# The first four slots of an expert stage loaded ahead of its table, and table work placed between its first steps

## The reference, cut to what matters

```python
logits = xf @ router_w.T
probs = jax.nn.softmax(logits, axis=-1)
_, top_idx = jax.lax.top_k(probs, TOP_K)
...
g = jnp.einsum('td,efd->tef', xf, gate_w)
u = jnp.einsum('td,efd->tef', xf, up_w)
h = jax.nn.silu(g) * u
h = h * comb_w[:, :, None]
y = jnp.einsum('tef,edf->td', h, down_w)
return y.reshape(B, S, D) + residual
```

## Time and profile before

| | |
|---|---|
| median of 3 runs | 547.34 us (545.66 to 548.88) |
| the profiled execution | 546.67 us, its span 545.0 us |
| TensorE busy | 482.8 us, 89% of the span |
| VectorE busy | 375.4 us, 69% |
| ScalarE busy | 304.6 us, 56% |
| GpSimd busy | 194.4 us, 36% |
| mean granted clock | 0.969 of 2.4 GHz |

### The profile page before, as it was taken

The page is one execution under the profiler, slowest core; times in us unless marked ns, Lnnn a source line. Parts: engine busy times, 40 slices in busy tenths (PEclk is TensorE's granted clock), DMA queues, the critical chain, the costliest instruction groups (busy, mean ns, idle before and its releaser), DMA issues.

```text
span 545.0 us, 12569 instructions
## 1 busy us (share of the span) xinstructions
PE 482.8 (89%) x3157; PEld 459.7 (84%) x3158; DVE 375.4 (69%) x1293; ACT 304.6 (56%) x773; POOL 194.4 (36%) x280
## 2 busy tenths in 40 slices
PE   1999998999788987799999999999999999999900
PEld 1999997877576876789999999999999999999800
DVE  4969996359979988857665665665665655665597
ACT  5484967548588885435444444444444444444473
POOL 1000000005667777764333333333333333333330
PEclk9999999999899998899999999999999999999965
DMA  8988123811333342262222222222222222225897
GB/s 304 413 351 356 24 93 94 313 45 44 106 109 118 95 128 78 91 173 72 79 75 68 78 75 68 76 77 68 76 76 68 76 77 68 71 81 154 258 354 232
DMA packets 61695, 71.67 MB, mean 132 GB/s; under 512 B 19057, under 2 KB 55730, under 8 KB 60642
## 3 DMA queue, kind: packets, MB, share of 16 engines
q1 hardware_dynamic: 49920, 51.43, 30.5%
q0 software_dynamic: 8592, 17.75, 9.0%
q10 hardware_dynamic: 3154, 2.15, 1.2%
HBM read 49.43 MB, written 21.86 MB: 131 GB/s over the span
## 4 chain that ended last, share of the span: by engine, by line
PE 73%; DVE 14%; DMA 5%; ACT 4%; issue 2%; ACTq 1%; SPq 0%; DVEq 0%; POOL 0%; POOLq 0%
PE bank L839 8%; PE pair L839 6%; PE bank L1089 5%; PE bank L1085 5%; PE bank L1088 5%; PE bank L1087 5%; PE bank L1086 5%; PE bank L1096 5%; PE pair L1105 4%; PE bank L1105 4%; PE pair L984 4%; PE pair L1074 3%; PE pair L988 3%; ACT yall L743 2%; DMA ydram<-ysb,dnow 2%; PE bank L918 2%
## 5 line engine op out<-in xcount | busy, mean ns | idle before, releaser
L776 POOL DMA_INDIRECT disp<-xf,posu x82 | 83.6, 1019 | 151.9 <-ACT xf L654 124.9
L1576 DVE TENSOR_TENSOR hh<-sg,bank 128x384 f32<-128x384 f32 x89 | 49.3, 554 | 99.5 <-ACT sg L724 99.5
L813 POOL DMA_INDIRECT ydram<-ysb,dnow x89 | 88.2, 991 | 70.6 <-DMA ydram<-ysb,dnow 36.5
L724 ACT ACTIVATE sg<-bank 128x384 f32<-128x384 f32 x89 | 43.7, 491 | 116.9 <-PE bank L1089 116.9
L1085 PE MATMUL bank<-wa,xh 128*128 x178 | 67.5, 379 | 0.0
L1089 PE MATMUL bank<-wa,xl 128*128 x178 | 60.4, 340 | 0.0
L1088 PE MATMUL bank<-wa,xh 128*128 x178 | 59.9, 337 | 0.0
L1086 PE MATMUL bank<-wa,xh 128*128 x178 | 59.7, 336 | 0.0
L1087 PE MATMUL bank<-wa,xl 128*128 x178 | 59.7, 336 | 0.0
L810 POOL COPY dnow<-dest 128x1 uint32 (+1 forms) x89 | 16.4, 185 | 105.9 <-DVE ysb L1586 96.5
L839 PE MATMUL bank<-wcT,imgT 128*128 128x193 f32 x240 | 42.5, 340 | 11.1 <-DMA imgT<-in_pixels 11.1
(11 more groups left out here) (263 smaller groups left out, 1170.9 us busy)
## 6 DMA issues: line engine op xcount, KB each, us to landing
xs<-disp SPq DMA_DIRECT2D x89, 96.0 KB, 1.9
band<-in_bands SPq DMA_DIRECT2D x4, 1536.0 KB, 12.1
yall<-ydram SPq DMA_DIRECT2D x7, 768.0 KB, 7.1
imgT<-in_pixels SPq DMA_DIRECT2D x4, 768.0 KB, 12.8
imgT<-in_pixels SPq DMA_DIRECT2D x2, 1536.0 KB, 16.2
hres<-in_text SPq DMA_DIRECT2D x1, 3072.0 KB, 26.1
wa<-in_gate_up_w SPq DMA_DIRECT2D x8, 384.0 KB, 8.5
ring<-in_gate_up_w SPq DMA_DIRECT2D x32, 96.0 KB
```

The costliest lines, as they stand in the source:

```text
L776: pool.indirect_dma_start(disp, bass.IndirectOffsetOnAxis(ap=posu[c % XBUF][:, 2 * j + k:2 * j + k + 1], axis=0), xfd[c % XBUF][:, j, :], None
L813: pool.indirect_dma_start(ydram, bass.IndirectOffsetOnAxis(ap=dnow[b][:], axis=0), ysb[r][:], None).then_inc(s_ys[b], 16)
```

## The change

VectorE takes a decision in chunk 9: where expert 0 has 512 rows ahead of that chunk, its first four slots are full and their places known (rows 0, 128, 256 and 384). It writes three numbers into `first` and gives table signal 1. SyncE reads them, waits for the scatters of chunks 0 to 8 (or, where the rows are fewer, for all and for signal 2), reads four row numbers and a guard from `pre` with an offset that it has read, and loads slots 0 to 3. Later it waits for the rest, reads four row numbers and a guard, and loads slots 4 to 7; then it waits for signal 4, reads all eight numbers of `ready`, and goes into the loop.

TensorE does the transposes of slot 0 ahead of its throw-away products, which are 10 in place of 40, and ahead of the table, now signal 2. Its wait for the whole table, at step 5, is now for signal 4.

VectorE keeps only the first part of the table ahead of the steps. The softmax's first half goes into step -2, `MID` and `ready` (signal 3) into steps 0 to 2, `FAR` (signal 4) into steps 3 and 4, the softmax's second half into steps 5 to 8. ScalarE does the exponential and a table load between the first steps too.

```diff
-WARM = (10, 40)
+FIRST_ROWS = DEPTH * P
+FIRST_CHUNK = 9
+OTHER = 8
+WARM = (10, 10)
...
# SyncE
             sp.wait_ge(s_tab, 1)
-            begin = [sp.alloc_register(f"slot_row{s}") for s in range(GUARDED)]
-            sp.reg_load(begin, tab[0:1, 0, 0:GUARDED])
-            free = [sp.value_load(guard[0:1, g:g + 1], ...) for g in range(GUARDED // DEPTH)]
+            tables = sp.value_load(first[0:1, 0:1], min_val=1, max_val=2)
+            other = sp.value_load(first[0:1, 1:2], min_val=0, max_val=OTHER)
+            full = landed(FIRST_CHUNK, 0, 0)
+            lowers = sp.value_load(first[0:1, 2:3], min_val=full, max_val=full + 16)
             for p in range(XBUF):
                 for j in range(4):
...
+                        sp.wait_ge(s_scat[p][j], lowers)
+            sp.wait_ge(s_tab, tables)
+            begin = [sp.value_load(pre[0:1, bass.ds(other + s, 1)], ...) for s in range(DEPTH)]
+            free = sp.value_load(pre[0:1, bass.ds(other + DEPTH, 1)], ...)
+            sp.wait_ge(s_pool, free)
...
+            for s in range(DEPTH):
+                if s == 2:
+                    sp.wait_ge(s_rt, CHUNKS)
+                load_slot(s, s, begin[s])
...
             sp.wait_ge(s_pool, POOL_SETUP + 1)
-            sp.wait_ge(s_tab, 3)
+            sp.wait_ge(s_tab, 4)
+            done = [[sp.value_load(ready[0:1, f, b:b + 1], ...) for b in range(2)]
+                    for f in range(len(MARKS) + 2)]
             with sp.Fori(0, (SLOTS - GUARDED) // DEPTH) as i:
...
# ScalarE
-            act.wait_ge(s_w, 1)
-            nc.scalar.activation(top8[...], top8[...], ACT.Exp).then_inc(s_exp, 1)
-            nc.scalar.preload_act_table_set("silu_and_others")
...
+                if isinstance(k, int) and k == -2:
+                    nc.scalar.preload_act_table_set("exp_and_others")
+                if isinstance(k, int) and k == -1:
+                    act.wait_ge(s_w, 1)
+                    nc.scalar.activation(top8[...], top8[...], ACT.Exp).then_inc(s_exp, 1)
+                    nc.scalar.preload_act_table_set("silu_and_others")
...
# TensorE
-            keep_busy(bank[0], WARM[1])
-            pe.wait_ge(s_lo, UNITS)
-            pe.wait_ge(s_tab, 1)
...
-                if isinstance(k, int) and k in (1, 5):
-                    pe.wait_ge(s_tab, 2 if k == 1 else 3)
+                if isinstance(k, int) and k == 5:
+                    pe.wait_ge(s_tab, 4)
...
+                if isinstance(k, int) and k == -2:
+                    keep_busy(bank[0], WARM[1])
+                    pe.wait_ge(s_lo, UNITS)
+                    pe.wait_ge(s_tab, 2)
...
# VectorE, places(c)
+                if c == FIRST_CHUNK:
+                    before = bank[6][0:1, RK:RK + 1]
+                    st.mark(v.tensor_scalar(first[0:1, 0:1], before, float(FIRST_ROWS), 1.0, ALU.is_lt, ALU.add))
+                    st.link(v.tensor_scalar(first[0:1, 1:2], before, float(FIRST_ROWS), float(OTHER), ALU.is_lt, ALU.mult))
+                    v.tensor_scalar(first[0:1, 2:3], first[0:1, 1:2], 16.0 / OTHER, 96.0, ALU.mult, ALU.add).then_inc(s_tab, 1)
...
# VectorE, between(k)
-                if k == 0:
+                if k == 3:
                     experts(*FAR)
-                if k == 1:
+                if k == 4:
                     rows_of(*FAR).then_inc(s_tab, 1)
...
-            pipeline(v, step, "xght", (2, 1, 0, -1), peel=5)
+            pipeline(v, step, "xght", (2, 1, 0, -1), peel=7)
```

## The result

The change makes the kernel 1.1% slower: 553.35 us (median of 4 runs, 550.75 to 554.74) against 547.22 us for the kernel before in the same session. The ratio is 1.0106, with a 95% interval of [1.0056, 1.0156]. The profiled execution took 552.51 us with a span of 550.9 us, 5.9 us over the span of before; its mean granted clock is 0.953 for 0.969.

The account below looks back on a forecast made before the run. Bound: forty throw-away products between chunks and slots, then a full TensorE. Slot 8's transposes 6.9 us later plus 1.7 us of low clock make +8.6 us on the profiled 546.67: 555.3 us, range 550.8 to 559.0.

Parts of the forecast that it names:

- Part 1 and 2: Front: early loads of slots 0 to 3, ten throw-away products for forty; slot 1's transposes at 233.5, 1.7 us earlier.
- Part 3: VectorE's work moved between the first steps: +0.1 us in all, at most +0.8.
- Part 4: TensorE at step 5 waits for signal 4, which VectorE gives after step 4's far rows: it stands 2.85 us.
- Part 5: SyncE's eight reads between signal 4 and slot 8's load take 5.2 us; TensorE stands 5.65 us more.
- The rival by which reads are nearly free: SyncE's eight reads pass at the rate of its moves, slot 8 only 0.5 us late: 548.4 us, chance 0.07.
- The failed term: Steps behind slot 8's start run at 1.2 GHz for a while: +1.7 us, 0 if the clock holds.
- a slow step 5 costs nothing: Low clock behind TensorE's first gap, at step 5: no further cost, since that step ends ahead of slot 8.
- the prediction's own signs: Wrong if slots 7 to 8 take under 5 us, clock is 1.00 through the gap, or first loads issue after 227.
- The last rival: SyncE's reads at 0.28 us plus 0.15 per check, 3.5 us for eight, and no clock loss: 551.9 us, chance 0.06.

Follow-up runs that it names:

- e2: The kernel after, with SyncE and TensorE waiting for signal 3 instead of 4, the eight reads staying ahead of slot 8: 545.44 us, ratio 0.9952.
- e3: e2 with the eight reads of `ready` moved behind the slot loop: 546.63 us, ratio 0.9974.
- e6: e2 with slots 8 to 11 written out and one pair of reads of `ready` behind each: 545.38 us, ratio 0.9954.
- e7: e6 with four row numbers in one register load, for slots 0 to 3 and again for 4 to 7: 543.28 us, ratio 0.9924.
- e8: e6 with no throw-away products behind slot 0's transposes: 544.46 us, ratio 0.9937.
- e9: e6 with forty throw-away products behind slot 0's transposes in place of ten: 552.38 us, ratio 1.0076.
- e11: e7 with no throw-away products behind slot 0's transposes: 542.83 us, ratio 0.9897.
- e10: e6 with the threshold of the decision in chunk 9 out of reach, so the first slots are loaded by signal 2: 551.83 us, ratio 1.0079.
- e12: The kernel before with ten throw-away products in place of forty between the counts and slot 0, nothing else: 548.40 us, ratio 1.0019.
- e1: The kernel after, with the eight reads of `ready` moved behind the slot loop: 549.85 us, ratio 1.0032.
- e4: The kernel before with its eight reads of `ready` all between the table wait and the slot loop: 547.57 us, ratio 0.9997.

## Why the prediction was right, and where it was not

The forecast of +8.6 us on the profiled execution became +5.8 (552.51 for 546.67): right in sign, inside the range of 550.8 to 559.0, and right on both mechanisms that make the loss, the wait at step 5 and the reads ahead of slot 8. It was wrong about the clock. Step by step:

| step | forecast | measured |
|---|---|---|
| SyncE's first slot DMA | 225.5 | 225.86 |
| x0 | 228.6 | 229.16 |
| twenty passes behind it | 4.5 us | 3.85 us |
| x1 | 233.5 | 233.29 |
| VectorE's moved work, x1 to x6 | +0.1 us | -0.4 us (14.18 for 14.57) |
| wait at step 5 | 2.85 us | 2.65 us (x6 to x7 2.81 longer) |
| signal 4 to slot 8's DMA | 6.2 us | 5.9 us |
| wait for slot 8 | 5.65 us | 3.57 us (x7 to x8 5.18 longer) |
| x8 against before | +6.9 us | +5.7 us |
| low clock behind x8 | +1.7 us | 0 |
| x8 to the end | 0 | +0.2 us |

**Part 1 and 2, the front**: right. The chain passes through the last scatter of chunk 8, issued at 219.76 and landed 2.35 us later, and then the five reads, as said. That the first DMA came within 0.4 us of the forecast is partly luck: the same scatter took 2.85 to 3.03 us to land in the traces of e2, e3, e6 to e9 and e11. (The prediction's terms give 225.2 for that DMA, 221.8 and 3.4; the 225.5 has 0.3 us that it doesn't name.) e10 and e12 add what the traces of before and after can't: the early decision alone carries the gain (5.8 us of x1 in e10), fewer products alone carry none (e12), and with the early loads forty products would lose 6.3 us of x1 (e9). Both parts are needed together.

**Part 3**: right that it is nearly free; before, slot 5 had waited 0.24 us for VectorE, which is gone.

**Part 4**: right to 0.2 us, on its mechanism too; in the timeline of VectorE the far rows run from 251.45 to 253.38, behind the `ysb` of step 4, as this piece shows:

```profile
251.17 0.36 DVE L1625 TENSOR_TENSOR ysb<-bank,ylo 128x192 f32<-128x192 f32 x1
251.45 0.61 DVE L1528 TENSOR_TENSOR tabf<-tabf,ct 128x440 f32<-128x440 f32 x1
...
253.19 0.19 DVE L1534 TENSOR_SCALAR tab<-slotf 128x55 int32<-128x55 f32 x1
```

e2 takes this wait away and with it the late start of the reads, and gains 1.5 points of ratio (1.0106 to 0.9952).

**Part 5**: right in mechanism, somewhat too large in size. A read costs 0.55 us behind another, not 0.62 to 0.7: eight take 4.4 to 4.5 us for 5.2. Entry and first DMA took 1.4 for 1.0, the landing 1.9 for 2.1. From signal to x8 are 8.38 us for 8.9. The rival by which reads are nearly free is refuted: 5.9 us in both the kernel after and e2, and 3.9 us of x8 in e1.

**The failed term is the clock's, +1.7 us.** I had the low stretch begin behind slot 8. It began behind the first gap instead: at x7 the clock was 0.52, and step 5 took 4.8 us for 3.14. The prediction had said that a slow step 5 costs nothing, since it ends ahead of slot 8, and that part holds: its 1.6 us more only shortened the wait for slot 8, 3.57 us where the load alone would have given 5.2. Behind x8 the clock stayed at 1.00. The prediction treated "a low stretch follows the longer gap" as settled by the earlier trace rows, with 0 us merely as an end of its range; the trace has a gap of 2.65 us that brought the clock down and one of 3.57 us that didn't. What differs ahead of them is that TensorE had worked at 1.00 for 18 us before the first, and only 1.6 us at 1.00 after a low stretch before the second; whether that decides was not tested and stays open. The Trainium skill, "TensorE: Matmul & The Clock Gate", section "HAM oscillation — how this bites in real kernels", has waits for DMA between groups of products throttle the array each time; the wait for slot 8 is such a wait, and there the trace disagrees. At x0 it can't tell: the clock had been low since 222.4, before TensorE began to wait for slot 0's load at 224.3. e1 turns the same low stretch into a cost: with no wait for slot 8 behind it, its step 5 of 4.7 us is on the path, which is why moving the reads away won 3.9 us at x8 rather than some 5.1 (there slot 8's second half, issued at 254.70, lands 2.0 us later).

By the prediction's own signs, too, the clock's term fails. It called itself wrong if the clock was 1.00 through the gap, and through slot 8's gap it was; the wait for slot 8 was to be over 5 us with 0.5 of the clock behind it, and was 3.57 us with 1.00. The other two signs of being wrong did not come: x8 minus x7 is 8.32 us, and the first DMA is at 225.86. The last rival, reads at the length of their rows and a clock that holds, gave 551.9 us and lies nearer to 552.51 than the forecast does. Its clock held behind x8, as measured; its price of a read, 0.43 us, was too low against 0.55.

Between +8.6 forecast and the +5.9 of the spans are 2.7 us: 1.7 in the clock, 0.5 in slot 8's chain, 0.5 in VectorE's work, 0.2 in the front, less 0.2 in the tail.

## What to carry to other kernels

When a signal is split into more steps, look at each waiter and ask which part it needs: here two waits took the last signal where the one before would do, and the whole loss lay in that. Work that a queue does between a signal and the next load (here eight register reads) is free as long as the signal is early (e4), and joins the critical path when the signal is late; spread it behind loads or read several numbers at once. And throw-away products are for time in which real work could not run: in the kernel before forty did better than ten by some 1 us (e12; 0.2 to 1.9 by the ratio's interval). Behind early data the first ten cost some 0.9 us (e6 against e8) and not their length of 4, for without them the low clock lasts until 235.5 instead of 233.2; sixty passes more cost their full length, 6.7 us (e9).

## What I had not expected of the hardware

- One register load of four numbers takes 0.30 to 0.33 us, as one of a single number does (0.27 to 0.41), and one of eight 0.74 us; three reads saved brought slot 0's DMA 1.9 us forward.
- A gap of 2.65 us on TensorE was followed by 3.1 us at the low clock, one of 3.57 us, 5 us later, by none.
- From x0 to the rise of the clock are 3.5 us in the kernel after and in e9, 4.4 in e7 and 5.4 in e10, all with a row of throw-away products behind x0; without such a row they are 4.6 in e12, 5.9 in e8 and 6.5 in e11. The kind of work alone does not order them, and what does was not tested.
- The last scatter of chunk 8 landed 2.35 us after its issue in the kernel after and 2.85 to 3.03 us after it in seven of its variants. That of the last chunk took 2.38 us in e10 and 3.20 in e12.
